# Cross-attention and routed experts on one core: row scores wait for one half of the stacked queries, value products before the next batch's first row scores, and a mask cast on ScalarE

## The chip, the cores and the metric

One core of a Trainium2 chip (trn2) runs the whole program. The time is device microseconds (us) of one execution. The kernel before took 427.91 us as the median of three runs (425.01, 427.91 and 429.54). Engines are called TensorE (PE), VectorE (DVE), ScalarE (ACT), GpSimd (POOL) and SyncE (SP).

## What is computed

`x` is 16 batches of 256 tokens by 128. A block of cross-attention with 16 heads of 8 columns reads a context of 64 rows for each batch, and a layer of 8 experts with two choices per token follows. All of it is fp32. The reference, cut to what matters here:

```python
x = x + xattn(layernorm(x), ctx, mask, Wq, Wk, Wv, Wo)
x = x + ffn(layernorm(x), gate_w, wi_gate, wi_up, wo)

# xattn
q = shape(H @ Wq, Lq) * dph ** (-0.5)
k = shape(T @ Wk, Lkv); v = shape(T @ Wv, Lkv)
scores = q @ k^T + (1.0 - mask)[:, None, None, :] * finfo.min
attn = softmax(scores)
out = (attn @ v) @ Wo

# ffn, for each of two choices k
expert = top_k_idx[:, k]; valid = position in expert < capacity
out += weight * down(silu(gate(x)) * up(x))      # of that expert
```

The mask is of integers, 0 for 48 to 64 leading positions of a batch and 1 for the others.

## The kernel before, in words

The program is written out engine by engine, with one in-order list of instructions for each and a semaphore for each dependency. It has three stages.

**Start.** SyncE loads the mask in two layouts (`MASKT`, `MASKR`), the context, `x` and the weights; ScalarE loads `WK`, the constants and `WQ`. VectorE casts `MASKT` to bf16 (`MASKB`, line 958), TensorE multiplies it by ones (line 829), and VectorE makes `ANY` of the counts (line 963). With `ANY` the context is masked (`mask_context`), split into a high and a low part (`context_hi`, `context_lo`), and projected to keys (`project_keys`). `ANYR` and `EXT` (lines 960, 961, 1187) are made of `MASKR` and give the mask's row of the keys. Around the mask's product stand `WARM0` = (4, 7) products whose result nobody reads (`keep_warm`). `project_values(0)` waits for `w_in` to reach 48, that is for `WV`, `WO` and `GATE`.

**Attention.** `over_steps` runs steps i = 0 to 19 on every engine at once. In a step, batches i-3 to i+3 are at different places of a pipeline. Of a batch b:

- `turn(b)` transposes the normalised tokens and `queries(b)` projects them; ScalarE and VectorE split them into `Q_HI` and `Q_LO`.
- `select(b, 0)` and `select(b, 1)` write the queries of two head groups each into one PSUM bank, and `stack_queries(b, h)` on ScalarE (line 535) copies half h of it into `QS`. `select(b, 1)` waits for the first copy. Each copy adds one to `qs_ready`.
- `row_scores(b, m)`, m = 0 to 3 (line 741), are two products each into banks 0 and 1. They serve only to find each row's maximum, which `row_max(b, m)` takes on VectorE (line 1024). m even reads half 0 of `QS`, m odd half 1. Before m = 0 TensorE waits for `qs_ready` 2b+2, so for both copies.
- `turn_maxima(b)` transposes the maxima and `keep_maxima(b)` on ScalarE (line 540) copies them beside the queries, as further rows of `QS`. After that `scores(b, j)` (line 764) give scores with the maximum already taken off, and `exps(b, j)` their exponentials (line 548).
- `sums(b)` and `values(b, 0)` (both line 773) are eight products each by 32 columns in two passes: the sums of the exponentials and the products on the values. ScalarE guesses the reciprocal (lines 559 and 564), VectorE corrects it (`errors` line 1030, `refine` line 1035), and `attention(b)` (line 1042) multiplies the two.
- `output`, `add_input`, `statistics2`, `moments2`, `variance2`, GpSimd's `inverse_deviation2` (line 415), `norm2` (line 1074), `turn2` (line 798) and `gate_logits` follow for batch i-2 or i-3, and then the routing of blocks of batches (`best`, `which`, `one_hot`, `rank`, and so on).
- GpSimd sends rows to their experts' places in memory (line 440), so many in each step as the table `SENDS` says. `MOMENTS` says in which steps (0, 1, 2, 3, 5, 7) VectorE also takes the moments of later batches, of which GpSimd makes inverse deviations (line 402), ahead of the step's sends.

At the end of step i TensorE's list has `sums(i-1)`, `turn_maxima(i)`, `select(i+1, 1)`, `row_scores(i+1, 0)`, `values(i-1, 0)`, and the next step begins with `turn(i+2)` and `turn2(i-2)`. ScalarE's list has there `stack_queries(i+1, 0)`, `log_sums`, `guesses`, `keep_maxima(i)`, `stack_queries(i+1, 1)`, and then `keep_turned(i+2)`. VectorE's has `errors(i-1)`, `norm2(i-2)`, `refine(i-1)`, `attention(i-1)`, `row_max(i+1, 0)` and, in some steps, `moments`.

**Experts.** Once all 64 sends have landed, the experts' rows are loaded and two experts are handled in each turn of a loop. Nothing in it is changed.

Of the kernel before, what the change touches and what calls it, by code (L numbers as in the profile page):

```python
# [23 lines left out]
ALU = mybir.AluOpType  # L24
ACT = mybir.ActivationFunctionType
AX = mybir.AxisListType
# [14 lines left out]
BIG = float(2.0 ** 127)  # L41
# [10 lines left out]
RT = 4  # L52
SENDS = {5: 4, 6: 3, 7: 5, 8: 3, 9: 5, 10: 4, 11: 5, 12: 5, 13: 5, 14: 5, 15: 4, 16: 4, 18: 12}
MOMENTS = {0: 2, 1: 3, 2: 4, 3: 5, 5: 6, 7: 7}
WARM0 = (4, 7)
WARM = 36
PLACED = 16 * 4 * HG

# [42 lines left out]
def program(nc, x, ctx, mask, maskt, wq, wk, wv, wo, gate, wgu, wdn, const, empty, zeros, out):  # L101
# [4 lines left out]
    with ExitStack() as stack:  # L106
# [3 lines left out]
        def sem(name):  # L110
            return stack.enter_context(nc.semaphore(name))
# [12 lines left out]
        def s1(name, shape, dt=F32):  # L124
            return sb(name, shape, dt, part1)
# [7 lines left out]
        MASKT = s1("maskt", [LK, B], I32)  # L133
        MASKB = s1("maskb", [LK, B], BF16)
        MASKR = s1("maskr", [B, LK], I32)
        ANYR = s1("anyr", [B, 1])
        EXT = s1("ext", [B, LK])
# [72 lines left out]
        const_in, maskt_in, maskr_in, w_in = sem("const_in"), sem("maskt_in"), sem("maskr_in"), sem("w_in")  # L210
# [5 lines left out]
        maskb_ready, count_full, any_ready = sem("maskb_ready"), sem("count_full"), sem("any_ready")  # L216
        anyr_ready, ext_step = sem("anyr_ready"), sem("ext_step")
# [9 lines left out]
        sel_full, qs_ready = sem("sel_full"), sem("qs_ready")  # L227
# [36 lines left out]
        def there(b):  # L264

            return 0 <= b < B

        def wait(eng, s, value):

            if not isinstance(value, int) or value > 0:  # L270
                eng.wait_ge(s, value)
# [210 lines left out]
        def _(act):  # L482
            act.dma_start(WK[:], wk).then_inc(wk_in, 16)
            act.dma_start(C[:], const).then_inc(const_in, 16)
            act.dma_start(WQ[:], wq).then_inc(wq_in, 16)
            nc.scalar.preload_act_table_set("natural_log_exp_and_others")
            act.wait_ge(wk_in, 16)
            nc.scalar.copy(WK_HI[:], WK[:]).then_inc(wk_hi_ready, 1)

# [178 lines left out]
        def _(pe):  # L668
# [6 lines left out]
            def keep_warm(n):  # L675

                for _ in range(n):
                    nc.tensor.matmul(ST[1][:], ONES[:], ONES[:].unsqueeze(1).to_broadcast([P, 4, P]), start=True, stop=True)
# [33 lines left out]
            def queries(b):  # L712

                pe.wait_ge(xt_ready, b + 1)
                nc.tensor.matmul(M0[:, 0:LQ], WQ[:], XT[b % 2][:], start=True, stop=True).then_inc(q_full, 1)
# [13 lines left out]
            def row_scores(b, m):  # L729

                t, bank = m // 2, m % 2
                if m == 0:
                    pe.wait_ge(qs_ready, 2 * b + 2)
                    if b < KBUF:
                        pe.wait_ge(ks_ready, b + 1)
                    else:
                        pe.wait_ge(keys_in[b // 2 % 2], PLACED * ((b - 2) // 4))
                wait(pe, m_ready, 4 * b + (m - 1))
                for gg in range(2):
                    g = 2 * bank + gg  # L740
                    mm = nc.tensor.matmul(MX[bank][:, gg * HG * LK:(gg + 1) * HG * LK],  # L741
                                          QS[b % 2][0:ONE_ROW + 1, g, t * P:(t + 1) * P], KS[0:ONE_ROW + 1, b % KBUF, g, :],
                                          start=True, stop=True)
                mm.then_inc(mx_full, 1)
# [23 lines left out]
            def values(b, what):  # L768

                for s in range(2):  # L770
                    for g in range(GROUPS):
                        w = V2[:, b, s * D + 32 * g:s * D + 32 * g + 32] if what == 0 else VMASK[:, s, g, :]
                        mm = nc.tensor.matmul((OUT_PS, DEN_PS)[what][32 * g:32 * g + 32, 0:LQ], w,  # L773
                                              PROBS[b % 2][:, g, s, :], start=(s == 0), stop=(s == 1))
                return mm
# [50 lines left out]
            pe.wait_ge(ones_set, 1)  # L826
            keep_warm(WARM0[0])
            pe.wait_ge(maskb_ready, 1)
            nc.tensor.matmul(ST[0][:, 0:B], ONES[0:LK, :], MASKB[:], start=True, stop=True).then_inc(count_full, 1)
            keep_warm(WARM0[1])  # L830
            for n in range(4):
# [15 lines left out]
            def step(i):  # L847
                if there(i + 1):
                    turn(i + 1)
                if there(i - 3):  # L850
                    turn2(i - 3)
                if there(i - 1):
                    scores(i - 1, 0)
                if there(i):
                    row_scores(i, 1)
                if i in (0, 1):
                    project_keys(2 * i + 4)
                if there(i + 1):
                    queries(i + 1)
                if there(i - 1):  # L860
                    scores(i - 1, 1)
                if there(i - 3):
                    gate_logits(i - 3)
                if there(i):
                    row_scores(i, 2)
                if i == 0:
                    project_values(2)
                if there(i - 1):
                    scores(i - 1, 2)
                if there(i):  # L870
                    row_scores(i, 3)
                if i == 0:
                    project_values(3)
                if there(i - 1):
                    scores(i - 1, 3)
                if there(i - 2):
                    output(i - 2)
                if there(i + 1):
                    select(i + 1, 0)
                if there(i - 1):  # L880
                    sums(i - 1)
                if i in (0, 1):
                    project_keys(2 * i + 5)
                if there(i):
                    turn_maxima(i)
                if there(i + 1):
                    select(i + 1, 1)
                    row_scores(i + 1, 0)
                if there(i - 1):
                    values(i - 1, 0).then_inc(pv_full, 1)  # L890
                if i in ROUTED:
                    rank(ROUTED[i], i)

# [60 lines left out]
        def _(dve):  # L954
            nc.vector.memset(V2[:, 0:4], 0.0).then_inc(v2_first, 1)
            nc.vector.memset(QS[0][ONE_ROW:ONE_ROW + 1, :, :].bitcast(F32), 1.0).then_inc(v2_first, 1)
            dve.wait_ge(maskt_in, 16)
            nc.vector.tensor_copy(MASKB[:], MASKT[:]).then_inc(maskb_ready, 1)
            dve.wait_ge(maskr_in, 16)
            nc.vector.tensor_reduce(ANYR[:], MASKR[:], AX.X, ALU.max).then_inc(anyr_ready, 1)  # L960
            nc.vector.tensor_scalar(EXT[:], MASKR[:], -1.0, BIG, ALU.add, ALU.mult).then_inc(ext_step, 1)
            dve.wait_ge(count_full, 1)
            nc.vector.tensor_scalar(ANY[:], ST[0][:, 0:B], 1.0, None, ALU.min).then_inc(any_ready, 1)

# [217 lines left out]
            mask_context(0)  # L1182
            dve.wait_ge(wk_hi_ready, 1)
            nc.vector.tensor_tensor(WK_LO[:], WK[:], WK_HI[:].bitcast(F32), ALU.subtract).then_inc(wk_lo_ready, 1)
            dve.wait_ge(anyr_ready, 1)
            dve.wait_ge(ext_step, 1)
            nc.vector.tensor_scalar(EXT[:], EXT[:], ANYR[:, 0:1], None, ALU.mult).then_inc(ext_step, 1)
# [200 lines left out]
```

## Time and profile before

| what | us |
|---|---|
| median of three runs | 427.91 (425.01 to 429.54) |
| the profiled execution | 425.72 |
| its span on the core | 423.9 |
| start, up to the first row scores | 20.3 |
| attention, up to the first row scores of batch 15 | 152.9 |
| attention's last steps and the last sends | 41 |
| experts | 210 |

| engine | busy, us | share of the span |
|---|---|---|
| PE | 364.0 | 86% |
| DVE | 251.7 | 59% |
| ACT | 194.6 | 46% |
| POOL | 229.6 | 54% |

The time of an execution is its span and 1.8 us around it. The busy shares are averages over stages: in the experts' stage TensorE is busy nearly without a break, in attention it is not.
### The profile page before, as it was taken

The page shows a single profiled execution, that of the slowest core. Times are in us where ns is not written, and L with a number is a line of the kernel's source. Part 1 is how long each engine was busy: PE and PEld are TensorE (multiplying, and loading weights), DVE is VectorE, ACT ScalarE, POOL GpSimd, SP SyncE. Part 2 cuts the span into 40 slices and gives each one's busy share as a digit, 9 for nine tenths or more (in the row PEclk, how much of TensorE's full clock was granted, in tenths as well). Part 3 has the DMA queues.
Part 4 walks back from the last instruction along what each step waited for, and adds up shares of the span by engine and source line. Part 5 has one row for each costly group of instructions (what it writes and reads, how often), then busy time and mean ns, then how long its engine had stood idle before and what let it go on. Part 6 is the DMA issues. An engine that isn't in the chain of part 4 may idle for free.

```text
span 423.9 us, 8967 instructions
## 1 busy us (share of the span) xinstructions
PE 364.0 (86%) x3012; PEld 313.7 (74%) x3012; DVE 251.7 (59%) x934; ACT 194.6 (46%) x438; POOL 229.6 (54%) x195
## 2 busy tenths in 40 slices
PE   5877788878788888875789999999999999999990
PEld 2565566656566566544579999999999999999980
DVE  6677776778676686676033556555555655555530
ACT  2566555656565565553033344334444433444320
POOL 6542331071864555577505638567483855838674
PEclk9999888989898898895889999999999999999996
DMA  8994101121222211112142353725446372544232
GB/s 252 306 320 166 15 6 16 30 54 39 57 65 53 84 44 46 47 57 66 47 126 20 28 155 33 163 28 90 102 38 157 31 160 28 97 92 39 26 32 25
DMA packets 41158, 34.33 MB, mean 81 GB/s; under 512 B 8336, under 2 KB 37520, under 8 KB 40976
## 3 DMA queue, kind: packets, MB, share of 16 engines
q1 hardware_dynamic: 26592, 23.40, 19.0%
q0 software_dynamic: 13568, 9.58, 16.4%
q10 hardware_dynamic: 960, 0.87, 0.7%
q8 instruction: 21, 0.34, 0.3%
q14 instruction: 17, 0.14, 0.1%
HBM read 21.12 MB, written 17.73 MB: 92 GB/s over the span
## 4 chain that ended last, share of the span: by engine, by line
PE 71%; ACT 11%; DVE 6%; issue 4%; POOL 4%; DMA 2%; POOLq 0%; SPq 0%; DVEq 0%; ACTq 0%
PE bank L913 16%; PE bank L671 10%; PE bank L773 9%; PE bank L673 9%; PE bank L672 9%; PE bank L741 5%; PE bank L764 3%; ACT qs L540 3%; POOL slots L440 3%; ACT qs L535 3%; PE bank L790 2%; PE bank L904 2%; ACT logd L559 1%; DVE mneg L1024 1%; ACT guess L564 1%
## 5 line engine op out<-in xcount | busy, mean ns | idle before, releaser
L472 POOL DMA_INDIRECT out<-ys,idx x80 | 125.5, 1569 | 83.8 <-DVE ys L1302 47.0
L1329 DVE TENSOR_TENSOR h<-sg,bank 128x256 f32<-128x256 f32 x160 | 66.2, 418 | 87.5 <-ACT sg L656 79.7
L656 ACT ACTIVATE sg<-bank 128x256 f32<-128x256 f32 x160 | 61.5, 385 | 108.3 <-PE bank L673 107.4
L671 PE MATMUL bank<-ex_hi,w_hi 128*128 128x256 f32 x320 | 96.0, 300 | 1.1 <-DVE ex_lo L1283 0.2
L673 PE MATMUL bank<-ex_lo,w_hi 128*128 128x256 f32 x320 | 89.7, 280 | 0.0
L672 PE MATMUL bank<-ex_hi,w_lo 128*128 128x256 f32 x320 | 89.7, 280 | 0.0
L913 PE MATMUL bank<-w_raw,h 128*128 128x128 f32 x640 | 78.0, 275 | 0.8 <-DVE h L1329 0.8
L913 PEld LDWEIGHTS bank<-w_raw,h 128*128 128x128 f32 x640 | 74.8, 192 | 1.0 <-DVE h L1329 1.0
L440 POOL DMA_INDIRECT slots<-rall,slot x64 | 62.8, 981 | 18.1 <-issue 17.7
L671 PEld LDWEIGHTS bank<-ex_hi,w_hi 128*128 128x128 f32 x320 | 61.0, 191 | 4.1 <-issue 2.5
L672 PEld LDWEIGHTS bank<-ex_hi,w_lo 128*128 128x128 f32 x320 | 61.0, 191 | 0.0
L673 PEld LDWEIGHTS bank<-ex_lo,w_hi 128*128 128x128 f32 x320 | 61.0, 191 | 0.0
L741 PE MATMUL bank<-ks,qs 97*128 97x256 f32 x128 | 30.8, 324 | 29.3 <-ACT qs L535 27.2
L1024 DVE TENSOR_REDUCE mneg<-bank 128x8 f32<-128x512 f32 x64 | 42.7, 686 | 7.8 <-PE bank L741 7.5
L741 PEld LDWEIGHTS bank<-ks,qs 97*128 97x128 f32 x128 | 21.2, 205 | 34.0 <-ACT qs L535 29.8
L548 ACT ACTIVATE probs<-bank 128x512 f32<-128x512 f32 x64 | 36.7, 598 | 7.3 <-PE bank L764 6.8
L415 POOL TENSOR_TENSOR rstd<-ve,half 128x2 f32<-128x2 f32 x16 | 12.0, 752 | 41.0 <-DVE ve L1068 40.9
L764 PE MATMUL bank<-qs,ks 113*128 113x256 f32 x128 | 33.0, 342 | 0.2 <-DVE at L1042 0.2
L402 POOL TENSOR_TENSOR rstd<-ve,half 128x4 f32<-128x4 f32 x8 | 8.5, 1059 | 41.9 <-DVE ve L998 41.9
L1302 DVE TENSOR_SCALAR ys<-bank,xl 128x128 f32<-128x128 f32 x80 | 24.1, 344 | 2.1 <-PE bank L913 2.1
L764 PEld LDWEIGHTS bank<-qs,ks 113*128 113x128 f32 x128 | 23.3, 214 | 1.6 <-DVE at L1042 0.4
L1283 DVE TENSOR_TENSOR ex_lo<-bank,ex_hi 128x512 fp32r<-128x512 f32 (+1 forms) x24 | 14.4, 600 | 16.4 <-ACT ex_hi L636 16.1
(122 smaller groups left out, 555.1 us busy)
## 6 DMA issues: line engine op xcount, KB each, us to landing
slots<-in_empty SPq DMA_DIRECT2D x8, 660.0 KB, 10.1
xl<-slots SPq DMA_DIRECT2D x7, 660.0 KB, 7.3
w_raw<-in_wgu SPq DMA_DIRECT2D x8, 512.0 KB, 3.8
w_raw<-in_wdn SPq DMA_DIRECT2D x8, 256.0 KB, 4.2
out<-X SPq DMA_DIRECT2D x16, 128.0 KB, 1.9
X<-in_x SPq DMA_DIRECT2D x3, 512.0 KB, 7.1
out<-ys,idx POOLq DMA_INDIRECT x80, 3.3
slots<-rall,slot POOLq DMA_INDIRECT x64, 2.3
```

The lines of the kernel that those rows point to most:

```text
L440: nc.gpsimd.indirect_dma_start(out=slots[:, :], out_offset=bass.IndirectOffsetOnAxis(ap=SLOT[:, tile, k:k + 1], axis=0), in_=RALL[:, tile, ...
L472: nc.gpsimd.indirect_dma_start(out=out[:, :], out_offset=bass.IndirectOffsetOnAxis(ap=IDX[v][:, j:j + 1], axis=0), in_=YS[c][:, t, :], in_ ...
L656: nc.scalar.activation(SG[m % 2][:], GATE_PS[m % 2][:, 0:2 * P], ACT.Silu).then_inc(sg_ready, 1)
L671: nc.tensor.matmul(ps, hi, m_hi, start=True, stop=False)
L672: nc.tensor.matmul(ps, lo, m_hi, start=False, stop=False)
L673: return nc.tensor.matmul(ps, hi, m_lo, start=False, stop=True)
L741: mm = nc.tensor.matmul(MX[bank][:, gg * HG * LK:(gg + 1) * HG * LK], QS[b % 2][0:ONE_ROW + 1, g, t * P:(t + 1) * P], KS[0:ONE_ROW + 1, b ...
L764: mm = nc.tensor.matmul(ST[j % 2][:, s * LQ:(s + 1) * LQ], KS[0:NROW, b % KBUF, j, s * P:(s + 1) * P], QS[b % 2][0:NROW, j, :], start=True ...
L773: mm = nc.tensor.matmul((OUT_PS, DEN_PS)[what][32 * g:32 * g + 32, 0:LQ], w, PROBS[b % 2][:, g, s, :], start=(s == 0), stop=(s == 1))
L913: mm = nc.tensor.matmul(Y_PS[n % 2][:, t * D:(t + 1) * D], H[n % 2][:, f, t * P:(t + 1) * P], W_RAW[v][:, 2 * F + f * D:2 * F + (f + 1) * ...
L1024: nc.vector.tensor_reduce(MNEG[b % 2][:, t, 1 + 8 * bank:9 + 8 * bank], MX[bank][:].rearrange("p (h k) -> p h k", k=LK), AX.X, ALU.max, ne ...
L1329: nc.vector.tensor_tensor(H[n % 2][:, f, :], SG[m % 2][:], UP_PS[m % 2][:, 0:2 * P], ALU.mult).then_inc(h_ready, 1)
```

## The change

Three things. `row_scores(b, 0)` waits for the first copy of the stacked queries alone, and `row_scores(b, 1)` for the second. In each step `values(i-1, 0)` stands ahead of `row_scores(i+1, 0)`. In the start, the cast of the mask moves from VectorE to ScalarE, `ANYR` and `EXT` move behind the masking of the context and the low part of the key weights, and one more unread product stands ahead of the keys.

```diff
-WARM0 = (4, 7)
+WARM0 = (4, 8)
...
             nc.scalar.preload_act_table_set("natural_log_exp_and_others")
+            act.wait_ge(maskt_in, 16)
+            nc.scalar.copy(MASKB[:], MASKT[:]).then_inc(maskb_ready, 1)
             act.wait_ge(wk_in, 16)
             nc.scalar.copy(WK_HI[:], WK[:]).then_inc(wk_hi_ready, 1)
...
             def row_scores(b, m):
 
                 t, bank = m // 2, m % 2
+                if m < 2:
+                    pe.wait_ge(qs_ready, 2 * b + 1 + m)
                 if m == 0:
-                    pe.wait_ge(qs_ready, 2 * b + 2)
                     if b < KBUF:
                         pe.wait_ge(ks_ready, b + 1)
...
                 if there(i + 1):
                     select(i + 1, 1)
-                    row_scores(i + 1, 0)
                 if there(i - 1):
                     values(i - 1, 0).then_inc(pv_full, 1)
+                if there(i + 1):
+                    row_scores(i + 1, 0)
                 if i in ROUTED:
                     rank(ROUTED[i], i)
...
-            dve.wait_ge(maskt_in, 16)
-            nc.vector.tensor_copy(MASKB[:], MASKT[:]).then_inc(maskb_ready, 1)
-            dve.wait_ge(maskr_in, 16)
-            nc.vector.tensor_reduce(ANYR[:], MASKR[:], AX.X, ALU.max).then_inc(anyr_ready, 1)
-            nc.vector.tensor_scalar(EXT[:], MASKR[:], -1.0, BIG, ALU.add, ALU.mult).then_inc(ext_step, 1)
             dve.wait_ge(count_full, 1)
...
             nc.vector.tensor_tensor(WK_LO[:], WK[:], WK_HI[:].bitcast(F32), ALU.subtract).then_inc(wk_lo_ready, 1)
+            dve.wait_ge(maskr_in, 16)
+            nc.vector.tensor_reduce(ANYR[:], MASKR[:], AX.X, ALU.max).then_inc(anyr_ready, 1)
+            nc.vector.tensor_scalar(EXT[:], MASKR[:], -1.0, BIG, ALU.add, ALU.mult).then_inc(ext_step, 1)
```

TensorE's list at the end of step 9 and the beginning of step 10, before. The batch whose row scores come is 10 (`qs0`), the products on values are of batch 8 (`probs0`), and the last rows shown are batch 10's second row scores (into bank 1).

```order
L726 MATMUL bank4<-q_lo,sel_lo 96x256
L741 MATMUL bank0<-ks,qs0 128x256 [waits m_ready,keys_in1,qs_ready]
L741 MATMUL bank0<-ks,qs0 128x256
L773 MATMUL bank3<-probs0,v2 32x256 x8
L709 MATMUL bank6<-C,xn1 128x128 [waits aug_ready,xn_ready]
L709 MATMUL bank6<-C,xn1 128x128
L798 MATMUL bank7<-C,rall 128x128 [waits x1_ready,rn_ready]
L798 MATMUL bank7<-C,rall 128x128
L764 MATMUL bank2<-qs1,ks 128x256 [waits p_ready,aug_ready]
L764 MATMUL bank2<-qs1,ks 128x256
L741 MATMUL bank1<-ks,qs0 128x256 [waits m_ready]
L741 MATMUL bank1<-ks,qs0 128x256
```

The same place in the changed kernel, whose lines are numbered two or three higher there:

```order
L728 MATMUL bank4<-q_lo,sel_lo 96x256
L776 MATMUL bank3<-probs0,v2 32x256 x8
L744 MATMUL bank0<-ks,qs0 128x256 [waits m_ready,keys_in1,qs_ready]
L744 MATMUL bank0<-ks,qs0 128x256
L711 MATMUL bank6<-C,xn1 128x128 [waits aug_ready,xn_ready]
L711 MATMUL bank6<-C,xn1 128x128
L801 MATMUL bank7<-C,rall 128x128 [waits x1_ready,rn_ready]
L801 MATMUL bank7<-C,rall 128x128
L767 MATMUL bank2<-qs1,ks 128x256 [waits p_ready,aug_ready]
L767 MATMUL bank2<-qs1,ks 128x256
L744 MATMUL bank1<-ks,qs0 128x256 [waits m_ready,qs_ready]
L744 MATMUL bank1<-ks,qs0 128x256
```

The eight products on values stand ahead of the first row scores, and the second row scores, six products later, now carry a wait for `qs_ready` too.

VectorE's list at the start, before:

```order
L956 MEMSET qs 1x1024
L958 CAST maskb<-maskt 64x16 [waits maskt_in]
L960 TENSOR_REDUCE anyr<-maskr 16x1 [waits maskr_in]
L961 TENSOR_SCALAR ext<-maskr 16x64
L963 TENSOR_SCALAR any<-bank 128x16 [waits count_full]
L970 TENSOR_TENSOR ctxm<-ctx,any 128x512 [waits any_ready,ctx_in0]
L1184 TENSOR_TENSOR wk_lo<-wk,wk_hi 128x384 [waits wk_hi_ready]
L1187 TENSOR_SCALAR ext<-ext,anyr 16x64 [waits ext_step,anyr_ready]
L976 TENSOR_TENSOR ctx_lo<-ctxm,ctx_hi 128x512 [waits ctx_hi_ready]
```

And in the changed kernel:

```order
L960 MEMSET qs 1x1024
L962 TENSOR_SCALAR any<-bank 128x16 [waits count_full]
L969 TENSOR_TENSOR ctxm<-ctx,any 128x512 [waits any_ready,ctx_in0]
L1183 TENSOR_TENSOR wk_lo<-wk,wk_hi 128x384 [waits wk_hi_ready]
L1185 TENSOR_REDUCE anyr<-maskr 16x1 [waits maskr_in]
L1186 TENSOR_SCALAR ext<-maskr 16x64
L1189 TENSOR_SCALAR ext<-ext,anyr 16x64 [waits ext_step,anyr_ready]
L975 TENSOR_TENSOR ctx_lo<-ctxm,ctx_hi 128x512 [waits ctx_hi_ready]
```

The cast is gone from this list, and the wait for `MASKR` stands behind the masked context.

## Rows read from the trace of the kernel before

**Rows 1.** The page: the chain that ended last, shares of the span by line

```profile
PE bank L913 16%; PE bank L671 10%; PE bank L773 9%; PE bank L673 9%; PE bank L672 9%; PE bank L741 5%; PE bank L764 3%; ACT qs L540 3%; POOL slots L440 3%; ACT qs L535 3%; PE bank L790 2%; PE bank L904 2%; ACT logd L559 1%; DVE mneg L1024 1%; ACT guess L564 1%
```

**Rows 2.** Waits, 29.8 to 173.5 us: who waited for whom, total, times, longest

```profile
PE bank L741 <- ACT qs L535: 26.4, 15, 1.8
...
DVE at L1042 <- PE bank L773: 23.7, 11, 2.6
...
DVE rall L1074 <- POOL rstd L415: 5.4, 2, 3.2
```

**Rows 3.** Timeline, PE, ACT and DVE, step 10: start, duration, line, [idle before]

```profile
122.43 0.50 PE L741 MATMUL bank<-ks,qs 97*128 97x256 f32 x2 [1.79 <-ACT qs L535]
...
122.86 1.07 PE L773 MATMUL bank<-probs,v 128*32 128x256 f32 x16
...
127.94 1.07 PE L773 MATMUL bank<-probs,C 128*32 128x256 f32 x16
...
129.52 0.28 PE L726 MATMUL bank<-q_lo,sel_lo 128*96 128x256 f32 x1
...
131.59 0.51 PE L741 MATMUL bank<-ks,qs 97*128 97x256 f32 x2 [1.79 <-ACT qs L535]
...
124.34 0.37 ACT L523 COPY xt<-bank 128x256 f32<-128x256 f32 x1 [1.96 <-PE bank L709]
...
128.05 0.58 ACT L535 CAST qs<-bank 96x512 fp32r<-96x512 f32 x1 [0.30 <-PE bank L726]
...
129.93 1.00 ACT L540 CAST qs<-bank 17x1024 fp32r<-17x1024 f32 x1
...
130.96 0.58 ACT L535 CAST qs<-bank 96x512 fp32r<-96x512 f32 x1
...
124.00 0.42 DVE L1042 SCALAR_TENSOR_TENSOR at<-bank,rneg 128x256 f32<-128x256 f32 x1 [1.95 <-PE bank L773]
...
130.84 0.42 DVE L1035 SCALAR_TENSOR_TENSOR rneg<-err,guess 128x256 f32<-128x256 f32 x1
```

**Rows 4.** Timeline, DVE and POOL, steps 6 and 8

```profile
82.64 0.42 DVE L1042 SCALAR_TENSOR_TENSOR at<-bank,rneg 128x256 f32<-128x256 f32 x1 [1.95 <-PE bank L773]
...
93.39 0.42 DVE L1042 SCALAR_TENSOR_TENSOR at<-bank,rneg 128x256 f32<-128x256 f32 x1
...
103.34 0.42 DVE L1042 SCALAR_TENSOR_TENSOR at<-bank,rneg 128x256 f32<-128x256 f32 x1 [1.95 <-PE bank L773]
...
105.84 1.01 POOL L402 TENSOR_TENSOR rstd<-ve,half 128x4 f32<-128x4 f32 x1 [5.79 <-DVE ve L998]
...
112.16 0.96 POOL L440 DMA_INDIRECT slots<-rall,slot  x1 [0.31 <-issue]
...
113.90 0.60 DVE L1074 TENSOR_SCALAR rall<-X,mv,rstd 128x128 f32<-128x128 f32 x2 [3.22 <-POOL rstd L415]
...
114.94 0.42 DVE L1042 SCALAR_TENSOR_TENSOR at<-bank,rneg 128x256 f32<-128x256 f32 x1
```

**Rows 5.** Stretches: length, busy us of each engine, granted clock, DMA

```profile
103.34:111.40 8.06, 6.08 (x54) 4.84 (x53) 7.27 (x38) 5.99 (x12) 4.47 (x5) 1.00 0.13 33
...
122.20:131.40 9.20, 7.38 (x72) 5.62 (x72) 7.21 (x33) 6.11 (x13) 5.59 (x6) 1.00 0.18 47
...
131.40:142.20 10.80, 9.03 (x77) 6.76 (x77) 7.43 (x37) 6.33 (x14) 4.64 (x5) 0.84 0.33 87
```

**Rows 6.** Line 1042, VectorE, 30 to 180 us: count, duration, first and last start

```profile
L1042 DVE SCALAR_TENSOR_TENSOR at<-bank,rneg x14: 424/425/425, 40.5 to 175.8; 128x256 f32<-128x256 f32 x14
```

**Rows 7.** Start: the cast, the gate's load (issue; size and us to landing), the values

```profile
3.32 1.74 DVE L958 CAST maskb<-maskt 64x16 bf16<-64x16 int32 x1
...
10.04 0.43 SPq L318 DMA_DIRECT2D gate<-in_gate  x1
...
gate<-in_gate SPq DMA_DIRECT2D x1, 4.0 KB, 4.3
...
14.44 1.09 PE L700 MATMUL bank<-wv,ctx 128*64 128x128 f32 x16
```

## The prediction

> **What bounds the kernel now.** I read the page first, then the waits of the attention stage, then one step on three engines, then the granted clock by stretches. In the chain of work that ended last, the experts' products stand first (lines 913 and 671 to 673), and nothing in the change touches them [rows 1]. The attention lines follow: row scores 741 with 5%, and on ScalarE line 540 with 3% and line 535 with 3% [rows 1]. A ScalarE copy on the chain of a stage whose big engine is TensorE says that TensorE waits for it.
>
> The waits say how much. Between 29.8 and 173.5 us TensorE waited 26.4 us for the copies of the stacked queries ahead of row scores, 15 times, at most 1.8 each, so once per step [rows 2]. VectorE waited 23.7 us for the products on values behind them [rows 2]. Step 10 shows the form of it: TensorE's `select` ends at 129.52 + 0.28 = 129.80, and the next row scores start at 131.59, 1.79 later, when the second copy (130.96 + 0.58 = 131.54) is there [rows 3]. The first copy was done at 128.05 + 0.58 = 128.63, and these row scores read no more than that half [rows 3]. The next copy could not be sooner: on ScalarE it stands behind the copy of the maxima at 129.93, 1.00 long [rows 3].
>
> **The change part by part, attention.** Nothing is added here but one wait. What goes is 1.79 us of an idle TensorE per step, if no other queue is late. I go through them at step 10, with 129.80 as the start.
>
> - TensorE: values 1.07, to 130.87; row scores 0.50, to 131.37; then `turn`, which needs the maxima's copy, ready at 130.93 [rows 3]. No wait. The second row scores come after three more pairs of products and find their copy (131.54) done. So TensorE's step is 9.16 (122.43 to 131.59) less 1.79 = 7.37 [rows 3].
> - ScalarE: it was idle 1.96 us before the copy of the turned tokens at 124.34 [rows 3]. That is 1.9 behind the row scores' old start of 122.43 [rows 3]; 1.79 sooner it is at 122.55, and ScalarE is free then from its own second copy, 0.05 before 122.43. It has 0.2 us to spare and would be next.
> - VectorE: `attention` waited 1.95 us for the values [rows 3]. Now the values are done at 130.87, before `refine` ends (130.84 + 0.42 = 131.26), so VectorE sets its time. From one `attention` (124.00) to there it is 7.26 us, and with one small reduction for the routing behind it about 7.4 [rows 3]. In step 8, which also has moments, the same stretch is 8.06 long [rows 5]. That work is in one row of instructions whose gaps are the engine's own, so the 8.06 is VectorE's floor there.
> - GpSimd: `norm2` needs its inverse deviation. In step 8 GpSimd gets the moments at 105.84, works 1.01, issues five sends (the last at 112.16) and only then makes the inverse deviation; VectorE waited 3.22 for it, up to 113.90, and `attention` was at 114.94, 11.60 after the last one at 103.34 [rows 4]. Step 6 has the same with four sends: 82.64 to 93.39, 10.75 [rows 4]. Both hang on VectorE's and GpSimd's own work since the last `attention`, none of which the change shortens. These two stretches stay as long as they are. In the other steps five sends and one inverse deviation take GpSimd 0.75 + 5 x 1.27 + 0.2 = 7.3, the 1.27 being (112.16 - 105.84 - 1.2) / 4 [rows 4]. That is just under 7.4.
>
> **The clock.** Steps of like content come in two lengths: 9.20 us at a granted clock of 1.00, and 10.80 at 0.84, a mean of the two levels [rows 5]. The level fell to 1.2 GHz eight times in the 13 stretches treated below, each time just behind the idle 1.79 us (one of the eight stands in the rows). A fall costs a step without moments 10.80 - 9.20 = 1.6 us, and less where VectorE's work covers it. With the idle time gone I take the level to stay at 2.4 GHz, except once behind one of GpSimd's two long waits: 1.6.
>
> **The sum.** `attention` started 14 times from 40.5 to 175.8, so 13 stretches take 135.3 us [rows 6]. Of them three have moments and no late GpSimd: 3 x 8.06 = 24.2. Two are GpSimd's: 10.75 + 11.60 = 22.35. Eight are left, at 7.5 (7.4 by VectorE, 7.4 by TensorE, 7.3 by GpSimd, and a tenth for their meeting): 60.0. Together 106.5, a gain of 28.8. Ahead of 40.5 lie the other two of the 15 waits, 26.4 - 13 x 1.79 = 3.1 us [rows 2, 3]; `turn` must wait for the maxima's copy there, so I take 2.8. Less 1.6 for the clock: 28.8 + 2.8 - 1.6 = 30.0.
>
> **The start.** The cast took VectorE 1.74 us for 64 x 16 numbers [rows 7]. No row shows it on ScalarE; its copies there go from 0.37 to 1.00 [rows 3], and I take 0.4, the nearest to so small a tile. `ANY` and the masked context no longer wait for `MASKR`, so the keys may start about 1 us sooner, and the eighth unread product lies in that wait. But `project_values(0)` started at 14.44, and the gate it waits for was issued at 10.04 and took 4.3, to 14.34 [rows 7]. SyncE's loads don't move. So all that is won ahead of that point is lost there, and I cost the start at nothing, with bounds from +0.4 (the ScalarE copy late in front of the key weights' cast) to -1 (where the gate lands sooner). The first row scores of batch 0 gain some tenths, which the second half of the context takes back.
>
> The steps after 176 have no row scores and no such wait; the 12 last sends in a row stay. I take nothing, from -1.5 to +1.5, since the clock may fall in other places.
>
> 30.0 off the profiled execution's 425.7 is 395.7. The median of the runs shown lies 2.2 higher, at 427.91, and the same 30.0 off it gives 397.9, which I forecast.
>
> A rule of the skill against this: the Trainium skill, SBUF — State Buffer, section "SBUF: two separate sides", says that VectorE and GpSimd share a pair of ports under a lock, and that the loser is blocked for the whole instruction. By it, each of 13 inverse deviations of 0.75 us could stand in VectorE's way once VectorE has no idle time: up to 9.8 us, which would leave a gain of 20. The trace bears out the lock at most in the 1.74 us of the cast; in the 8.06 us without an idle VectorE, GpSimd was busy 4.47 beside it, so its price is already in my 8.06 [rows 5, 7].
>
> **The rivals.**
>
> 1. *The clock keeps falling.* For: TensorE's steps keep dozens of small products and short gaps, and only one fast step stands between slow ones. Against: every fall followed the gap that goes. Eight falls instead of one cost 7 x 1.6 = 11.2: 409. The Trainium skill, TensorE: Matmul & The Clock Gate, section "HAM oscillation", says that short idles between groups of products alone can keep the level swinging; that is this rival. Chance 0.17.
> 2. *GpSimd or VectorE sets a longer pace.* For: GpSimd at 7.3 and VectorE at 7.4 stand a tenth under the step. If each meets the other late, the eight plain stretches are like those with moments, 8.1: 8 x 0.6 = 4.8 less, and a tenth or two in the others: 403. Chance 0.13.
> 3. *The wait only moves* to `turn` or to the second row scores, since ScalarE's chain from the sums to the second copy is unchanged. Against: the 0.2 us to spare at step 10. It would leave the 3 us of the start: 425. Chance 0.04.
> 4. *Slower: TensorE at 1.2 GHz through most of attention.* At half the clock half the work is done, so h us at that level cost h/2 against a stage without falls, which is 28.8 + 2.8 = 31.6 shorter than now. The change turns slower once 2 x 31.6 = 63 us of the stage are at it; before, some 8 x 3.2 = 26 us were (1.6 us lost is half of 3.2). With 80 us it is 40 - 31.6 = 8.4 slower: 436. A denser TensorE could meet a limit that the trace never shows. Chance 0.03.
> 5. *More than forecast:* no fall at all and shorter last steps, 30 + 1.6 + 1.5 and 2 for the plain stretches at TensorE's 7.2: 393 or less. Chance 0.03.
>
> The forecast has 0.60. A measurement of this kernel can tell about 1% from no change. Faster by over 1%: the forecast and rivals 1, 2 and 5, 0.93. Within 1%: rival 3, 0.04. Slower: 0.03. The range goes from 390 (rival 5 and the start's last microsecond) to 411 (rival 1 and two more for the plain stretches).
>
> **What would show it.** In the trace of the changed kernel, TensorE's wait for line 535 ahead of row scores should be gone from the attention steps, and VectorE's wait for the values with it. `attention` should start 7.3 to 7.6 us after the last one in plain steps, 8.0 to 8.3 in those with moments, and still 10.7 and 11.6 in steps 6 and 8, with `norm2` behind GpSimd. The granted clock should be 1.00 in nearly all stretches from 40 to 145 us. The values of the start should still begin near 14.4. Wrong would be: a new wait of 1 us or more per step ahead of `turn` or `scores`, the clock at 0.84 in every other step, or GpSimd's inverse deviation late in more than two steps.

## The result and the profile after

The changed kernel takes 398.32 us (median of 4 runs, 396.81 to 400.82) where the kernel before takes 427.97 beside it: a ratio of 0.932, with a 95% interval of 0.925 to 0.940. The forecast was 397.9. The profiled execution is 396.81 long, its span 395.0, against 425.72 and 423.9 before.

The page's chain by line, of the changed kernel:

```profile
PE bank L917 18%; PE bank L673 11%; PE bank L675 9%; PE bank L674 9%; POOL slots L440 6%; PE bank L776 4%; DVE mneg L1023 3%; PE bank L744 2%; PE bank L767 2%; PE bank L908 2%; PE bank L793 1%; DMA maskr<-in_mask 1%; POOL rstd L415 1%; DVE rall L1073 1%; PE bank L727 1%
```

Line 744 (the row scores, line 741 in [rows 1]) has gone from 5% to 2%, and ScalarE's two copies (lines 540 and 535 there) have left the row. What comes instead is GpSimd's sends, line 440, with 6% where there were 3%: the time that is left in attention is partly theirs.

The waits from 38 to 146 us of the changed kernel:

```profile
DVE rall L1073 <- POOL rstd L415: 5.4, 2, 3.2
...
PE bank L801 <- DVE rall L1073: 4.7, 2, 2.9
...
PE bank L744 <- DVE mneg L1023: 3.3, 5, 0.7
```

The two first rows of [rows 2] have no counterpart: TensorE waits nowhere for the stacked queries, and VectorE nowhere for the values. The third one stands unchanged, 5.4 us in two waits, and TensorE now waits behind it (4.7 us, line 801 is `turn2`). TensorE's wait for the row maxima is 3.3 us in five; in the kernel before it is 1.8 in three from 40 to 176 us, so it has grown by little.

One step without moments, TensorE, ScalarE and VectorE, the same instructions as in [rows 3]:

```profile
114.58 1.07 PE L776 MATMUL bank<-probs,v 128*32 128x256 f32 x16
...
115.58 0.51 PE L744 MATMUL bank<-ks,qs 97*128 97x256 f32 x2
...
116.07 0.41 PE L711 MATMUL bank<-C,xn 128*128 128x128 f32 x2
...
112.89 0.58 ACT L537 CAST qs<-bank 96x512 fp32r<-96x512 f32 x1 [0.31 <-PE bank L728]
...
114.78 1.00 ACT L542 CAST qs<-bank 17x1024 fp32r<-17x1024 f32 x1
...
115.81 0.58 ACT L537 CAST qs<-bank 96x512 fp32r<-96x512 f32 x1
...
116.52 0.37 ACT L525 COPY xt<-bank 128x256 f32<-128x256 f32 x1
...
115.69 0.42 DVE L1034 SCALAR_TENSOR_TENSOR rneg<-err,guess 128x256 f32<-128x256 f32 x1
...
116.21 0.42 DVE L1041 SCALAR_TENSOR_TENSOR at<-bank,rneg 128x256 f32<-128x256 f32 x1
```

The values (line 776) run at once, and the row scores (744) behind them at 115.58 need only the first copy, done at 112.89 + 0.58. The transposes (711) follow at 116.07. ScalarE's second copy ends at 115.81 + 0.58 = 116.39, ahead of the row scores that read it (116.78), and the copy of the turned tokens starts at 116.52: its idle time was 1.96 and is 0.13. VectorE's `refine` ends at 116.11 and `attention` starts at 116.21, with the small reduction for the routing between them and no wait.

The stretches from one `attention` to the next, for steps 5, 6, 8 and 9:

```profile
62.85:69.85 7.00, 7.00 (x73) 5.37 (x71) 6.86 (x29) 5.84 (x13) 0.76 (x1) 1.00 0.13 21
...
69.85:80.40 10.55, 8.01 (x81) 5.98 (x79) 8.31 (x42) 6.61 (x14) 6.73 (x7) 1.00 0.24 62
...
87.41:99.01 11.60, 8.02 (x81) 5.98 (x79) 8.30 (x43) 6.61 (x14) 7.48 (x8) 1.00 0.20 52
...
99.01:108.97 9.96, 9.96 (x71) 7.84 (x70) 7.43 (x31) 5.89 (x12) 4.73 (x6) 0.66 0.21 59
```

In step 5 TensorE is busy 7.00 us of 7.00. Steps 6 and 8 are 10.55 and 11.60 long, with TensorE busy 8.0 in each. Step 9 is busy throughout too, but at a granted clock of 0.66: it took 9.96, where the other steps without moments take 7.2 on the average.

The end of step 8, GpSimd, VectorE, TensorE:

```profile
97.21 0.72 POOL L415 TENSOR_TENSOR rstd<-ve,half 128x2 f32<-128x2 f32 x1
...
97.97 0.60 DVE L1073 TENSOR_SCALAR rall<-X,mv,rstd 128x128 f32<-128x128 f32 x2 [3.23 <-POOL rstd L415]
...
98.63 0.44 PE L801 MATMUL bank<-C,rall 128*128 128x128 f32 x2 [2.86 <-DVE rall L1073]
```

VectorE waits 3.23 us for the inverse deviation and TensorE 2.86 us behind it, as [rows 4] has it for VectorE. There the clock falls. At the end of step 6 TensorE waits 1.81 us in the same way, and the clock stays.

And the start of the changed kernel (the cast; the gate's load, its time to landing; the first values):

```profile
3.52 0.20 ACT L488 CAST maskb<-maskt 64x16 bf16<-64x16 int32 x1
...
11.17 0.43 SPq L318 DMA_DIRECT2D gate<-in_gate  x1
...
gate<-in_gate SPq DMA_DIRECT2D x1, 4.0 KB, 3.9
...
15.20 1.09 PE L702 MATMUL bank<-wv,ctx 128*64 128x128 f32 x16 [1.09 <-issue]
```

### The profile page after: what moved, and what is told of

Its sections match the earlier page's. It is cut to its first block, busy times and chain, and to the rows that moved or that the text cites. A ratio compares the mean times of both kernels' runs of the same rounds, so it can differ in the third digit from the quotient of the medians.

```text
span 395.0 us, 8984 instructions
## 1 busy us (share of the span) xinstructions
PE 354.4 (90%) x3013; PEld 309.2 (78%) x3013; DVE 248.8 (63%) x933; ACT 194.0 (49%) x439; POOL 229.5 (58%) x195
## 4 chain that ended last, share of the span: by engine, by line
PE 65%; DVE 11%; POOL 9%; issue 6%; ACT 4%; DMA 3%; POOLq 1%; SPq 0%; DVEq 0%; ACTq 0%
PE bank L917 18%; PE bank L673 11%; PE bank L675 9%; PE bank L674 9%; POOL slots L440 6%; PE bank L776 4%; DVE mneg L1023 3%; PE bank L744 2%; PE bank L767 2%; PE bank L908 2%; PE bank L793 1%; DMA maskr<-in_mask 1%; POOL rstd L415 1%; DVE rall L1073 1%; PE bank L727 1%
## 5 line engine op out<-in xcount | busy, mean ns | idle before, releaser
L744 PE MATMUL bank<-ks,qs 97*128 97x256 f32 x128 | 29.9, 316 | 3.5 <-DVE mneg L1023 3.3
L767 PE MATMUL bank<-qs,ks 113*128 113x256 f32 x128 | 31.1, 326 | 0.2 <-DVE at L1041 0.2
L744 PEld LDWEIGHTS bank<-ks,qs 97*128 97x128 f32 x128 | 20.0, 193 | 10.8 <-issue 5.9
L1285 DVE TENSOR_TENSOR ex_lo<-bank,ex_hi 128x512 fp32r<-128x512 f32 (+1 forms) x24 | 14.4, 599 | 16.4 <-ACT ex_hi L638 16.1
L767 PEld LDWEIGHTS bank<-qs,ks 113*128 113x128 f32 x128 | 21.6, 199 | 1.7 <-ACT probs L550 0.5
```

What stands on the lines that cost most here:

```text
L767: mm = nc.tensor.matmul(ST[j % 2][:, s * LQ:(s + 1) * LQ], KS[0:NROW, b % KBUF, j, s * P:(s + 1) * P], QS[b % 2][0:NROW, j, :], start=True ...
```

## The experiments

They ran on several chips. Beside the first four, the ninth to the eleventh and the twelfth the kernel before took some 453 us, beside the fifth to the eighth 426.95. Ratios are therefore taken against runs on the same chip, and the verdicts on steps from the profiles. What is different on the slower chips is told at the fourth experiment. The whole change never ran on a slower chip. Its two changes of attention bring 3.1% there together, and 2.3 and 2.7% each alone, where the whole change brings 7% on a chip like the first.

**1 and 6. The waits alone.** The products on values stay behind the row scores; each half of the row scores waits for its own copy.

```diff
                 if there(i + 1):
                     select(i + 1, 1)
-                if there(i - 1):
-                    values(i - 1, 0).then_inc(pv_full, 1)
-                if there(i + 1):
                     row_scores(i + 1, 0)
+                if there(i - 1):
+                    values(i - 1, 0).then_inc(pv_full, 1)
                 if i in ROUTED:
```

> The changed kernel with the old order: the first row scores stand ahead of the products on values again, but wait for the first copy alone. My theory (the wait for the second copy is what cost, and its 1.79 us go wherever values stand): TensorE's step is as short as in the changed kernel. VectorE gets the values 0.5 us later, at about 1.5 us behind the end of select instead of 1.07, some 0.1 to 0.2 behind its own refine, so 1 to 2 us in all: 399 to 400 against 398.3. Rival (the order is what counts, because attention waits behind the row scores): VectorE, which sets the pace, loses the full 0.5 us in each of 15 steps, and the time is 404 or more.

It took 439.99 us, ratio 0.977 (0.966 to 0.988). On the chip like the first one:

> The first experiment again (old order, new waits), beside the whole change on one chip. My theory: 1 to 2 us over the whole change. Rival (the order counts by 0.5 us in each of 15 steps): 6 us or more over it.

It took 397.05 us (ratio 0.928, 0.922 to 0.934), beside 399.68 for the whole change. The time is not above the whole change, where 1 to 2 us more were expected, so the waits bring all of the gain that can be measured. The stretches from `attention` to `attention` are the same to 0.1 us (7.24, 7.47, 7.35, 6.96 and 7.19 for steps 10 to 14, against 7.24, 7.57, 7.36, 6.96 and 7.30). I had expected VectorE to get the values a tenth or two too late; the small reduction between `refine` and `attention` covers that.

**2 and 7. The order alone.** The values stand ahead, and the first row scores wait for both copies.

```diff
-                if m < 2:
-                    pe.wait_ge(qs_ready, 2 * b + 1 + m)
                 if m == 0:
+                    pe.wait_ge(qs_ready, 2 * b + 2)
```

> The changed kernel with the old wait: values stand ahead, but the first row scores wait for both copies. My theory: the values' 1.07 us fill the gap and 0.7 us of it are left, in the waits as TensorE line 744 behind ScalarE's copy, about 0.7 x 15 = 10 us. The gain is 15 x 1.07 = 16 us and what the clock gives. If a gap of 0.7 us no longer lets the granted clock fall, 6 to 10 us more: 402 to 406. If it still falls every other step: 411 to 413. Rival (VectorE is the pace and a 0.7 us gap on TensorE is hidden beside it): 399 to 400.

It took 437.92 us, ratio 0.973 (0.961 to 0.985). On that chip the order alone, the waits alone and both (experiment 3) can't be told apart.

> The second experiment again (new order, old wait). My theory: some 0.7 us of wait per step stay on TensorE; 4 to 8 us over the whole change if the granted clock no longer falls, 13 to 15 if it does. Rival (hidden beside VectorE): within 1.5 us of the whole change.

It took 405.88 us (ratio 0.947, 0.942 to 0.953), 6.2 over the whole change. TensorE's values and row scores of one step, its wait for the second copy between 27 and 150 us, and its wait behind GpSimd's late inverse deviation in step 6:

```profile
131.34 1.07 PE L775 MATMUL bank<-probs,v 128*32 128x256 f32 x16
...
133.20 0.50 PE L743 MATMUL bank<-ks,qs 97*128 97x256 f32 x2 [0.79 <-ACT qs L537]
...
PE bank L743 <- ACT qs L537: 11.6, 14, 1.5
...
85.96 0.69 PE L800 MATMUL bank<-C,rall 128*128 128x128 f32 x2 [0.96 <-DVE rall L1072]
```

The values fill 1 us of the gap and 0.79 stays in a step, 14 waits and 11.6 us in all. Of what was expected, the loss of 4 to 8 us came: the granted clock fell at GpSimd's two waits, but in no step that had a gap of 0.79 us alone. The first of the two falls began at 85.7, in a wait of only 0.96 us with a gap of 0.79 us 1 us ahead of it. So order and wait are two ways to the same idle time. The wait alone takes all of it. The order alone leaves 11.6 of the 26.4 us [rows 2] and brings 21.1 us of time where the whole change brings 27.3, and together they bring no more than the wait.

**3. The two changes of attention, with the old start.**

```diff
-WARM0 = (4, 8)
+WARM0 = (4, 7)
...
-            act.wait_ge(maskt_in, 16)
-            nc.scalar.copy(MASKB[:], MASKT[:]).then_inc(maskb_ready, 1)
             act.wait_ge(wk_in, 16)
...
+            dve.wait_ge(maskt_in, 16)
+            nc.vector.tensor_copy(MASKB[:], MASKT[:]).then_inc(maskb_ready, 1)
...
```

> The kernel before with the two changes of the attention stage, and its start as it was. My theory (the start is worth nothing, since the first values wait for the gate's load): 398 to 399, the same as the changed kernel within 1 us. Rival (the start brought about a microsecond of the gain): 399.3 or more.

It took 436.87 us, ratio 0.969 (0.954 to 0.984), on a chip where its theory's figure could not be met. The whole change did not run on that chip, so the time decides nothing on the start.

**4. The start alone.** The kernel before with the cast on ScalarE, the mask's row later and the eighth product.

```diff
-WARM0 = (4, 7)
+WARM0 = (4, 8)
...
+            act.wait_ge(maskt_in, 16)
+            nc.scalar.copy(MASKB[:], MASKT[:]).then_inc(maskb_ready, 1)
             act.wait_ge(wk_in, 16)
...
-            dve.wait_ge(maskt_in, 16)
-            nc.vector.tensor_copy(MASKB[:], MASKT[:]).then_inc(maskb_ready, 1)
...
```

> The kernel before with the changes of the start alone (the cast on ScalarE, the mask's row later, one more unread product). My theory: the same as before, 427 to 428.4, with the values at the start beginning no earlier than the gate's landing. Rival (the start loses: in the changed kernel's profile its first values began 0.76 us later than before): 428.7.

450.72 us, ratio 0.997 (0.991 to 1.003): no change that can be told, as expected, though the interval would also hold a gain of 4 us.

What makes these chips slower shows in the third experiment's profile, in step 6 (ScalarE's second copy and its copy of the turned tokens, TensorE's queries; and ScalarE's wait in total from 30 to 190 us; the releaser "remote" is one that the kernel's own queues don't show):

```profile
79.22 0.58 ACT L535 CAST qs<-bank 96x512 fp32r<-96x512 f32 x1 [1.12 <-remote]
...
83.94 0.37 ACT L523 COPY xt<-bank 128x256 f32<-128x256 f32 x1 [4.14 <-remote]
...
84.37 0.50 PEld L715 LDWEIGHTS bank<-xt,wq 128*128 128x128 f32 x2 [3.77 <-ACT xt L523]
...
ACT xt L523 <- remote: 15.6, 5, 4.1
```

ScalarE stands still for 1.12 and then 4.14 us after what it needs is there, and TensorE 3.77 us behind it. The four stretches before that step are 8.10, 8.03, 8.29 and 7.10 long, no longer than on the first chip; from the first of GpSimd's sends (73.42 us of that span) the stretches are 10.2 to 15.3. Such waits stand in all eight profiles from slower chips and in none of the six others, and nowhere before the sends or in the experts' stage. So they come with the sends, or with what else begins at that step. What they are stays open; nothing was tried on them.

**5. The whole change once more.**

> The changed kernel itself, beside the parts of it in the same call, since the first four experiments ran on a chip where the kernel before took 453.75 us and nothing says yet what the whole change takes there. My theory: where before takes some 428, this takes 398 (ratio 0.93). On a chip as in the first call: 436 to 438, the same as the two changes of attention alone, because stalls that no queue of the kernel explains fill the steps there. Rival for that: the change's gain is the same 30 us on every chip, 424.

399.68 us (396.14 to 403.97), ratio 0.927 (0.921 to 0.933), as expected for such a chip. Its profiled execution was longer than the first one by 2.5 us of span. The granted clock was at the lower level for 6.8 us in step 7 and 10.2 in step 9, each time at one of GpSimd's waits (TensorE idle for 1.87 and 2.86 us; the stretches are 9.93 and 10.89), where the first profile had 6.8 us behind the second wait alone.

**8. Sends first.** In steps 5 and 7 GpSimd makes the inverse deviation of the later moments after the step's sends.

```diff
-                if i in MOMENTS:
+                if i in MOMENTS and i not in SENDS:
                     inverse_deviation(MOMENTS[i])
...
                 for n in range(first, first + SENDS.get(i, 0)):
                     send(n)
+                if i in MOMENTS and i in SENDS:
+                    inverse_deviation(MOMENTS[i])
```

> The changed kernel with GpSimd's list turned round in steps 5 and 7: the step's sends stand ahead of the inverse deviation of the later moments instead of behind it. My theory (GpSimd's late inverse deviation holds steps 6 and 8 at 10.55 and 11.60 us): both fall to about 8.1, the wait of norm2 on GpSimd goes, and with it the one fall of the granted clock that made step 9 9.96 instead of 7.4. That is 2.45 + 3.5 + 2.5 = 8.5 us less than the whole change, 390 where that takes 398. Rival A (the five sends are what takes the time, in whatever order): no change. Rival B (the clock's fall has another cause): 6 us less, and the fall stays.

It took 388.09 us (387.29 to 389.35), ratio 0.908 (0.903 to 0.912). GpSimd at the end of step 7 and in step 8, and `attention` on VectorE:

```profile
90.19 0.96 POOL L440 DMA_INDIRECT slots<-rall,slot  x1 [0.30 <-issue]
...
91.17 1.05 POOL L402 TENSOR_TENSOR rstd<-ve,half 128x4 f32<-128x4 f32 x1
...
92.49 0.73 POOL L415 TENSOR_TENSOR rstd<-ve,half 128x2 f32<-128x2 f32 x1 [0.28 <-DVE ve L1069]
...
86.32 0.42 DVE L1043 SCALAR_TENSOR_TENSOR at<-bank,rneg 128x256 f32<-128x256 f32 x1
...
94.61 0.42 DVE L1043 SCALAR_TENSOR_TENSOR at<-bank,rneg 128x256 f32<-128x256 f32 x1
```

The last of five sends is over before the moments' inverse deviation at 91.17, and the one that `norm2` needs runs at 92.49, for whose input GpSimd now waits 0.28 us itself. Steps 6 and 8 take 8.29 each (86.32 to 94.61). From 27 us of the span to the end of the 13 stretches the clock doesn't fall once. The 13 stretches take 98.98 us, 8.35 less than in the changed kernel's first profile, as expected; the time is 11.6 under the whole change's on the same chip, since that also pays for a second fall, as the fifth experiment's profile has it. Rivals A and B fall. On the slower chips the same turn brings nothing that can be told: 0.969 without it (experiment 3) and 0.969 with it (experiment 9).

**9. The old start, with the sends first.** The edit is the third experiment's, on the eighth.

> Sends ahead of the late inverse deviations, the two changes of attention, and the start as it was before. Against the eighth experiment (388.1 us, sends first with the new start) it tells what the start's changes are worth where nothing else swings. My theory: the same within 0.7 us, since the first values wait for the gate's landing either way. Rival (the start brought a microsecond): 389.1 or more.

**10. The gate's load ahead of the large loads of x, with the sends first.**

```diff
+            sp.dma_start(WO[:], wo).then_inc(w_in, 16)
+            sp.dma_start(GATE[:], gate).then_inc(w_in, 16)
             for q in range(1, 4):
                 sp.dma_start(X[:, 8 * q:8 * q + 8, :], x_t[:, 8 * q:8 * q + 8, :]).then_inc(x_in[q + 1], 16)
-            sp.dma_start(WO[:], wo).then_inc(w_in, 16)
-            sp.dma_start(GATE[:], gate).then_inc(w_in, 16)
```

> The eighth experiment with the loads of WO and GATE issued ahead of the three large loads of x. My theory (after the change the first values wait some 1.1 us for the gate's landing): they begin at about 13.5 to 14.2 instead of 14.7, and the time is 0.5 to 1 us below the eighth experiment's 388.1: 387.1 to 387.6. Rival (the later x loads, pushed back, or the positions' transposed tokens hold the start instead): 388.1 or more.

**11. The old order, with the sends first.** The edit is the first experiment's, on the eighth.

> The eighth experiment with the old order: the first row scores ahead of the values, each waiting for its own copy. My new theory, after the sixth experiment came out no slower than the whole change: moving the values is worth nothing in either direction, as TensorE has no wait between the two, and VectorE gets both before it needs them: 388.1 within 0.8. Rival (it is worth the 1 to 2 us that I expected, hidden before by the clock's falls): 389.1 to 390.

These three ran on a slower chip: 434.35, 429.94 and 432.35 us, with ratios of 0.969 (0.960 to 0.978), 0.963 (0.955 to 0.970) and 0.964 (0.955 to 0.973). The ranges of the single runs overlap, so the times decide neither the start nor the order to the microsecond, and the figures that were expected belong to another chip. The profile of the tenth shows what had held the start (the gate's issue, the first values, the first row scores):

```profile
4.97 0.43 SPq L316 DMA_DIRECT2D gate<-in_gate  x1
...
12.30 1.09 PE L704 MATMUL bank<-wv,ctx 128*64 128x128 f32 x16
...
17.45 0.47 PE L746 MATMUL bank<-ks,qs 97*128 97x256 f32 x2 [0.19 <-POOL ks L406]
```

The first values begin at 12.30 instead of 14.4 to 15.4, sooner than the 13.5 to 14.2 that were expected, and the row scores are now released by GpSimd's spreading of the keys (17.45, against 19.66 in the eleventh). The first `attention` instruction stands at 35.2 us of the span, against 39.5 in the eleventh. Not all of these 4 us are the gate's. In the tenth the key products follow each other at 0.23 us from the first on; in the eleventh they begin at 0.43, and from 22.5 to 26.0 us its granted clock is 0.53. The first experiment has its keys at 0.23 as the tenth, no such fall and the gate late, and its first `attention` at 38.3, so the gate's part is about 3 us.

**12. The same once more.**

> The tenth experiment once more, since its call ran on a chip where the kernel before took 453 us. There its first attention instruction stood at 35.2 us of its span, against 39.5 in the eleventh and 39.2 in the eighth. Theory: those 4 us stay to the end where no unexplained stalls follow: 384 to 385.5 where before takes 427 (ratio 0.90). Rival (the earlier start is taken back by GpSimd's first sends or by the clock): 387 or more, ratio 0.907 as in the eighth.

Again a slower chip: 429.3 us, ratio 0.953 (0.946 to 0.961). Its profile gives the other half of the start (the first product of the keys, the first values):

```profile
9.42 0.74 PE L675 MATMUL bank<-ctx_hi,wk_hi 128*96 128x512 f32 x1 [2.03 <-DVE ctx_lo L977]
...
15.21 1.09 PE L704 MATMUL bank<-wv,ctx 128*64 128x128 f32 x16
```

The gate was issued at 4.96 and landed 5.4 later, at 10.36, long before it was needed. But TensorE ran the keys at the lower level, 0.43 us from one product to the next against 0.23 in the tenth, and reached the values at 15.21 by itself; the first `attention` stood at 40.8. So an early gate is worth up to some 3 us at the first `attention`, in an execution in which the clock is up by then, and nothing in one in which it is not. Whether it lowers the median is open: no run of it fell on a chip like the first.

## Why the prediction was right

**The wait.** TensorE's idle 1.79 us per step went as the forecast had it, without a new wait in front of `turn` or of the second row scores. The reason given holds: the second copy ends (116.39) before TensorE has done the products that stand ahead of its use (116.78). ScalarE keeps 0.13 us (forecast 0.2). Experiments 6 and 7 show which edit did it: the wait.

**The three kinds of stretches.** Those with moments took 8.10, 8.04 and 8.64, together 24.8 (forecast 24.2). GpSimd's two took 10.55 and 11.60, together 22.2 (22.35). The eight plain ones took 60.4 (60.0), with the clock's fall of step 9 in them; without that step they are 50.4 for seven, 7.2 each and not 7.5. I had added a tenth for engines meeting late and taken TensorE's 7.37 as a floor; it goes down to 6.96. In step 9 the fall cost 9.96 - 7.2 = 2.8, where I had put 1.6 for one fall: the lower level lasted 6.8 us and not the 3.4 of a fall in the kernel before. Stretches and fall together were to be 108.1 and are 107.3 (38.07 to 145.40). That this comes within 1% is in part luck: shorter plain steps and a dearer fall offset each other, and in the fifth experiment's profile, with two falls, the same stretches take 111.4.

**The clock.** In the old 13 stretches it fell nine times, not the eight of the prediction: the ninth begins at 173.3, 0.1 us behind the wait of step 14. That makes rival 1 dearer by one fall, 1.6 us, and leaves the forecast as it is. In the new stretches it fell once, at a wait of GpSimd's, and the eighth experiment takes that wait away and the fall with it. How long an idle time is doesn't decide alone: 1.79 us went with a fall in nine of 13 stretches, 1.81 us (step 6 of the changed kernel) with none, 1.87 us at the same place with one (experiment 5), and 0.79 us with one only where 0.96 us more followed (experiment 7).

Rival 1 did not come. The rule beside it stands in the Trainium skill, TensorE: Matmul & The Clock Gate, section "A second HAM failure mode: psum-queue depth-cycling", behind the section that the prediction names. It is not put to the test here. The short gaps that rival 1 counts on do not stand in the rows: in step 10 before, TensorE is busy 7.38 of 9.20 us [rows 5], so that 1.79 of the 1.82 left are the one wait, and in the changed kernel's plain steps the profile shows no idle time at all.

**GpSimd's two waits.** They stayed as forecast, and the eighth experiment shows them to be a matter of order, worth 8.35 us of the 13 stretches against the first profile and 11.6 of the median, falls of the clock included.

**The shared ports.** By the rule of the Trainium skill (SBUF — State Buffer, section "SBUF: two separate sides") up to 9.8 us were to go. In attention nothing of it is seen: over all fourteen profiles VectorE's two scalings of tokens (`xn`) take 0.58 us together, both in the 136 places where GpSimd's inverse deviation runs beside them and in the 22 where none does. At the start the trace agrees with the rule. GpSimd's memory set and VectorE's cast in the kernel before, and the cast in the ninth experiment:

```profile
1.49 3.54 POOL L389 MEMSET kc<- 32x2048 f32 x2
...
3.32 1.74 DVE L958 CAST maskb<-maskt 64x16 bf16<-64x16 int32 x1
...
3.44 1.63 DVE L962 CAST maskb<-maskt 64x16 bf16<-64x16 int32 x1 [0.20 <-DMA maskt<-in_maskt]
```

The casts begin at different times and end at 5.06 and 5.07, just behind the memory set (5.03 and 5.04). The third experiment has the same (3.49 + 1.58 = 5.07). No run moved the memory set, so that it holds the cast back is read from these times alone.

**The start.** Forecast at nothing. On ScalarE the cast takes 0.20 us, against 1.74 [rows 7], and `ANY` is ready 3 us sooner. The keys start at 8.5 to 9.5 us with the new start and at 9.6 to 10.7 with the old, so about the 1 us sooner that was forecast. But in the nine profiles with the new start and the gate's load late TensorE then stands idle for 0.8 to 2.4 us and starts the values 0.05 to 0.13 us behind the gate's landing: 11.17 + 3.9 = 15.07 and 15.20 in the changed kernel. In the three with the old start it has no idle time there and starts them 0.1 to 0.4 us behind the landing (14.34 and 14.44 before), so that keys and gate held the values about equally. The tenth experiment moved the gate and the values came. At the first row scores the old start with the new attention stands at 20.12 and 20.19 us (experiments 3 and 9), the new start at 19.5 to 20.2 (the changed kernel in both its profiles, and experiment 8), so it brings 0 to 0.7 us there. Attention began 2.4 us sooner than before and not 2.8; the gate was issued at 10.04 in the profile of the kernel before and at 10.4 to 11.3 in the eleven others that have it late, whatever their start. A gain or loss of the start in the median was not measured.

**The end.** From the last of the 14 `attention` instructions to the end of the span it is 249.6 us against 248.1 before: 1.5 were lost, the edge of what I had allowed, 1.2 of it in step 15, which ran at a clock of 0.77 and took 7.46 against 6.23. In the profiles of experiments 5, 6 and 8 it runs at 1.00 and takes 6.2. The span's gain is 2.4 + 28.0 - 1.5 = 28.9. The median moved by 29.65.

**The chip.** The prediction has no term for it. On a slower chip the two changes of attention, together or alone, took 436.87 to 439.99 us, 14 to 17 less than the kernel before, with stalls of another kind in the steps. That the result comes from a chip like that of the trace is luck.

## What to carry to other kernels

A semaphore wait on a count of two copies where the instruction reads only the first is worth more here than the moved instructions (29.9 us against 21.1), and needs no new order: split the wait by what is read. After an idle time has gone, look at the waits of other queues that stay; here GpSimd's list held two steps of 13, and turning two entries round brought 11.6 us more on such a chip, and nothing that can be told on a slower one. A prediction by engine (what each one's list takes from one point of a step to the same point of the next, and which needs the longest) came within 1% on the stage, where the sum of waits alone (26.4 us) would not have named GpSimd's two steps or the clock.

## What the runs showed beyond that

- TensorE pays for idle time twice, once in the time itself and once in the clock behind it. In the kernel before 1.79 us idle in a step went with nine falls in 13 stretches, of 3.4 us each. At GpSimd's two waits (TensorE idle for 0.96 to 2.86 us) falls lasted 3.4 to 10.2 us in the profiles of the whole change and of its parts. What sets their length was not tried. The changed kernel's times go from 396 to 404, and its longer runs have the lower mean clock (0.938 at 404, 0.955 at 396); with the sends first it is 387.3 to 389.4.
- On some chips the kernel before is 26 us slower. In the one pair of profiles that allows it (the kernel before on the first chip, the start alone on a slower one) 21 of 25 us lie in the 13 stretches of attention. From the first indirect sends on, ScalarE and VectorE stand still for up to 4.8 us for something that no queue of the kernel shows.
- A cast of 64 x 16 numbers on VectorE took 1.58 to 1.74 us and ended each time with GpSimd's memory set beside it; on ScalarE it took 0.20 us beside the same memory set.
